# The last stage of a two-layer model: token order of the expert weights, and which engine normalises, takes the powers and splits the activations

## The reference, cut to what matters

```python
x = x + _L1_ffn_ref(_layernorm(x, axis=-1), ...)

shared = silu(x @ shared_w_gate.T) * (x @ shared_w_up.T) @ shared_w_down.T   # 352 wide
shared = shared * sigmoid(x @ shared_gate_w.T)
logits = x @ gate_w.T                          # 16 experts
rw, sel = top_k(softmax(logits), 2)
rw = rw / rw.sum(axis=-1, keepdims=True)
combine = zeros((N, 16)).at[arange(N)[:, None], sel].set(rw)
g, h = split(einsum('nd,edf->nef', x, w_gate_up), 2)      # 64 wide each
out = einsum('nef,efd,ne->nd', silu(g) * h, w_down, combine) + shared
```

## Time and profile before

| | us |
|---|---|
| median of 3 runs (2034.19 to 2035.87) | 2034.31 |
| the profiled execution, device time | 2034.19 |
| its span in the trace | 2032.0 |
| of that, the last stage from its first normalisation | 1781.3 to the end |
| ScalarE, busy in the whole span | 1498.5 |
| GpSimd, busy in the whole span | 899.9 |

### The profile page before, as it was taken

The page is one execution under the profiler, slowest core; times in us unless marked ns, Lnnn a source line. Parts: engine busy times, 40 slices in busy tenths (PEclk is TensorE's granted clock), DMA queues, the critical chain, the costliest instruction groups (busy, mean ns, idle before and its releaser), DMA issues. The chain is left out here.

```text
span 2032.0 us, 51069 instructions
## 1 busy us (share of the span) xinstructions
PE 1710.1 (84%) x13415; PEld 1396.7 (69%) x13415; DVE 1594.2 (78%) x5015; ACT 1498.5 (74%) x4147; POOL 899.9 (44%) x1335
## 2 busy tenths in 40 slices
PE   3599999999999999972530569999999889887997
PEld 3499999999999999951420246666666566575775
DVE  4798888888888888846688759999999778874664
ACT  3488888888888888846576369999999688763553
POOL 1554444444444444404155114444444277724554
PEclk8699999999999999985665779999999889978998
DMA  4366666666666666620000039999999710034654
GB/s 138 89 164 166 162 160 160 160 158 159 161 163 163 160 159 161 158 63 0 0 0 0 0 84 248 247 249 246 245 247 247 179 33 0 2 48 72 99 99 103
DMA packets 224923, 261.66 MB, mean 129 GB/s; under 512 B 25144, under 2 KB 178268, under 8 KB 224720
## 3 DMA queue, kind: packets, MB, share of 16 engines
q1 hardware_dynamic: 223366, 258.64, 51.7%
q10 hardware_dynamic: 1194, 1.58, 0.3%
q0 software_dynamic: 288, 0.56, 0.1%
HBM read 88.19 MB, written 4.74 MB: 46 GB/s over the span
## 5 line engine op out<-in xcount | busy, mean ns | idle before, releaser
L777 ACT ACTIVATE a_prob<-a_neg,a_nmax 128x289 f32<-128x289 f32 x512 | 268.0, 529 | 1.3 <-DVE a_nmax L704 1.0
L839 PE MATMUL a_out<-a_probT,a_xn 128*128 128x256 f32 x1024 | 265.4, 383 | 3.9 <-DMA a_probT<-a_blocks 2.3
L1709 ACT ACTIVATE b_prob<-b_neg,b_nmax 128x257 f32<-128x257 f32 x512 | 261.1, 516 | 4.9 <-DVE b_nmax L1660 4.5
L670 POOL TENSOR_TENSOR a_xn<-a_z,g 128x256 f32<-128x256 f32 x128 | 93.9, 734 | 383.5 <-DVE a_z L738 383.5
L829 PE MATMUL a_score<-a_xnT,a_qT 128*128 128x290 f32 x1536 | 252.6, 314 | 1.1 <-DVE a_qT L749 1.1
L704 DVE CUSTOM_DVE_ANT_0 a_neg<-a_score,a_bias 128x289 f32<-128x289 f32 x512 | 210.6, 458 | 40.5 <-PE a_score L829 36.0
L785 ACT ACTIVATE a_prob<-a_prob,a_rinv 128x289 f32<-128x289 f32 x512 | 232.1, 529 | 1.7 <-DVE a_rinv L754 1.7
L829 PEld LDWEIGHTS a_score<-a_xnT,a_qT 128*128 128x128 f32 x1536 | 221.9, 190 | 8.0 <-issue 1.6
L1660 DVE CUSTOM_DVE_ANT_0 b_neg<-b_score,b_bias 128x257 f32<-128x257 f32 x512 | 188.9, 422 | 32.7 <-PE b_score L1800 17.6
L839 PEld LDWEIGHTS a_out<-a_probT,a_xn 128*128 128x128 f32 x1024 | 176.8, 192 | 19.1 <-DMA a_probT<-a_blocks 2.9
L715 DVE STREAM_TRANSPOSE a_blocks<-a_prob 128x1024 f32<-128x1024 f32 x128 | 159.4, 1245 | 25.1 <-ACT a_prob L785 18.4
(11 more groups left out here) (480 smaller groups left out, 4551.7 us busy)
## 6 DMA issues: line engine op xcount, KB each, us to landing
a_probT<-a_blocks SPq DMA_DIRECT2D x512, 192.0 KB, 3.4
b_probT<-b_blocks SPq DMA_DIRECT2D x256, 256.0 KB, 4.7
a_raw<-in_ctx SPq DMA_DIRECT2D x128, 128.0 KB, 3.0
b_raw<-in_ctx SPq DMA_DIRECT2D x64, 256.0 KB, 4.2
m_wide<-expert_weights SPq DMA_DIRECT2D x128, 128.0 KB, 6.7
a_kept<-keep SPq DMA_DIRECT2D x32, 257.0 KB, 3.4
b_kept<-keep SPq DMA_DIRECT2D x32, 257.0 KB, 4.7
b_v_rows<-ctx_tail_values SPq DMA_DIRECT2D x32, 256.0 KB, 4.7
```

What stands on the lines that cost most here:

```text
L777: nc.scalar.activation(prob[:, par, grp, 0:KEYS0], neg[:, grp, :], ACT.Exp, bias=nmax[:, par, grp:grp + 1], scale=-1.0, accum_out=rsum[:, ...
L839: nc.tensor.matmul(out_ps[:, half, 0:2 * P], xn[:, j, kt, :], probT[:, u, 2 * half:2 * half + 2, kt, :], start=(kt == 0), stop=False)
L1709: nc.scalar.activation(prob[:, (j + 5) % 4, grp, :], neg[:, par, grp, :], ACT.Exp, bias=nmax[:, par, grp:grp + 1], scale=-1.0, accum_out=r ...
```

## The change

It does six things in `moe1`:

- Columns of `y` keep the tile order (no `by_batch` / `by_tile`), and so does `expert_weights`, now [17, 4096] in place of [4, 17, 1024]. A load of one expert's chunk reads one run of 512 floats in place of 4 runs of 128. A store writes, for each row and tile, a run of 32 floats, in place of one run for each row.
- DVE normalises all four tiles of each chunk; ACT normalises none, and `offset` goes.
- The low half of `y` is made by POOL, from `yT` and `y[:, HI]`, in place of DVE from PSUM. ACT's next copy into the same `yT` buffer waits for it; PE's next turn into the bank waits for ACT's copy alone.
- The exponentials become powers, e^gap and (1/e)^logit, on POOL (`gap_powers`, `gate_powers`), in place of ACT's `exps`.
- POOL takes the powers of part 0 after the low half of chunk 3, the gate powers of part 1 after its first `hidden[LO]`, and the gap powers of part 1 after its sixth.
- PE waits before the main loop until all `y[:, HI]` are written.

```diff
                 def store_weights(part):
                     tiles = tiles_of(part)
                     sp.wait_ge(comb_turned[part], 1)
-                    for i in range(BPT):
-                        sp.dma_start(k.comb_dram[i, :, tiles.start * L:tiles.stop * L],
-                                     combT[i * L:i * L + COLS, tiles, :].rearrange("e t l -> e (t l)")).then_inc(comb_stored, 16)
-                    sp.wait_ge(comb_stored, (part + 1) * BPT * 16)
+                    for i in range(P // L):
+                        sp.dma_start(k.comb_dram[:, tiles.start * P:tiles.stop * P].rearrange("e (t i l) -> e t i l", i=P // L, l=L)[:, :, i],
+                                     combT[i * L:i * L + COLS, tiles, :]).then_inc(comb_stored, 16)
+                    sp.wait_ge(comb_stored, (part + 1) * (P // L) * 16)
...
-                            sp.dma_start(wide[e * E_FF:(e + 1) * E_FF, p % 4, :].rearrange("p (i q) -> p i q", i=BPT),
-                                         weights_of(2 * p + e, c, E_FF)).then_inc(wide_loaded[p % 4], 16)
+                            sp.dma_start(wide[e * E_FF:(e + 1) * E_FF, p % 4, :],
+                                         k.comb_dram[2 * p + e:2 * p + e + 1, ds(c * CH, CH)].broadcast_to([E_FF, CH]))\
+                                .then_inc(wide_loaded[p % 4], 16)
...
-                    wait(pe, y_lo, c - 1)
+                    wait(pe, y_hi, c - 1)
...
-                def exps(part):
-                    tiles = tiles_of(part)
-                    act.wait_ge(chain[part], 12)
-                    nc.scalar.activation(powers[:, 0, tiles], gap[:, tiles], ACT.Exp)
-                    nc.scalar.activation(powers[:, 1, tiles], logits[:, tiles, E_N], ACT.Exp, scale=-1.0).then_inc(exped[part], 1)
...
+                    wait(act, y_lo, c - 1)
                     nc.scalar.activation(yT[:, c % 2, :], ln_ps[c % 2][:], ACT.Copy).then_inc(copied, 1)
-                    nc.scalar.activation(by_batch(y[:, HI, c * CH:(c + 1) * CH]), by_tile(ln_ps[c % 2][:]), ACT.Copy).then_inc(y_hi, 1)
+                    nc.scalar.activation(y[:, HI, c * CH:(c + 1) * CH], ln_ps[c % 2][:], ACT.Copy).then_inc(y_hi, 1)
...
+                def gap_powers(part):
+                    tiles = tiles_of(part)
+                    pool.wait_ge(chain[part], 12)
+                    nc.gpsimd.tensor_tensor(powers[:, 0, tiles], base[:, 0:1].broadcast_to([P, tiles.stop - tiles.start]), gap[:, tiles],
+                                            ALU.pow).then_inc(gap_power[part], 1)
...
+                for c in range(CHUNKS):
+                    pool.wait_ge(y_hi, c + 1)
+                    nc.gpsimd.tensor_tensor(y[:, LO, c * CH:(c + 1) * CH], yT[:, c % 2, :], y[:, HI, c * CH:(c + 1) * CH],
+                                            ALU.subtract).then_inc(y_lo, 1)
+                    if c == 3:
+                        gate_powers(0)
+                        gap_powers(0)
...
                     if op == 12:
-                        dve.wait_ge(exped[part], 1)
+                        dve.wait_ge(gap_power[part], 1)
+                        wait_apart(k, dve, gate_power[part], 1)
...
-                        nc.vector.tensor_tensor(by_tile(total[:]), by_batch(expert_ps[:]), by_batch(shared[:]), ALU.add).then_inc(total_ready, 1)
+                        nc.vector.tensor_tensor(total[:], expert_ps[:], shared[:], ALU.add).then_inc(total_ready, 1)
```

More of the change, by code:

```diff
@@ L10 @@
+import math
 from contextlib import ExitStack
@@ L2114, in moe1 @@
         powers = sb("m_powers", [P, 2, TILES])
-        offset = sb("m_offset", [P, TILES])
+        base = sb("m_base", [P, 2])
         comb, combT = sb("m_comb", [P, TILES, L]), sb("m_combT", [P, TILES, L])
@@ L2125, in moe1 @@
         shared, total = sb("m_shared_out", [P, CH]), sb("m_total", [P, CH])
-        z_act, z_dve, z_turned, copied, y_hi, y_lo, routed, gathered, offset_ready, comb_zeroed = (
-            sem(f"m_{n}") for n in ("z_act", "z_dve", "z_turned", "copied", "y_hi", "y_lo", "routed", "gathered", "offset_ready", "comb_zeroed"))
-        chain, exped, comb_turned = ([sem(f"m_{n}{part}") for part in range(2)] for n in ("chain", "exped", "comb_turned"))
+        z_ready, z_turned, copied, y_hi, y_lo, routed, gathered, base_ready, comb_zeroed = (
+            sem(f"m_{n}") for n in ("z_ready", "z_turned", "copied", "y_hi", "y_lo", "routed", "gathered", "base_ready", "comb_zeroed"))
+        chain, gap_power, gate_power, comb_turned = ([sem(f"m_{n}{part}") for part in range(2)] for n in (
+            "chain", "gap_power", "gate_power", "comb_turned"))
         comb_stored = sem("m_comb_stored")
@@ L2184, in store_weights @@
                     sp.wait_ge(comb_turned[part], 1)
-                    for i in range(BPT):
-                        sp.dma_start(k.comb_dram[i, :, tiles.start * L:tiles.stop * L],
-                                     combT[i * L:i * L + COLS, tiles, :].rearrange("e t l -> e (t l)")).then_inc(comb_stored, 16)
-                    sp.wait_ge(comb_stored, (part + 1) * BPT * 16)
-                def weights_of(e, c, rows):
-                    return k.comb_dram[:, e, ds(c * P, P)].unsqueeze(0).broadcast_to([rows, BPT, P])
+                    for i in range(P // L):
+                        sp.dma_start(k.comb_dram[:, tiles.start * P:tiles.stop * P].rearrange("e (t i l) -> e t i l", i=P // L, l=L)[:, :, i],
+                                     combT[i * L:i * L + COLS, tiles, :]).then_inc(comb_stored, 16)
+                    sp.wait_ge(comb_stored, (part + 1) * (P // L) * 16)
                 def chunk(c, u):
@@ L2196, in chunk @@
                         wait_apart(k, sp, shared_taken, c - 1)
-                    sp.dma_start(wide_share[:, u, :].rearrange("p (i q) -> p i q", i=BPT), weights_of(E_N, c, P)).then_inc(share_loaded[u], 16)
+                    sp.dma_start(wide_share[:, u, :], k.comb_dram[E_N:E_N + 1, ds(c * CH, CH)].broadcast_to([P, CH]))\
+                        .then_inc(share_loaded[u], 16)
                     for p in range(PAIRS):
@@ L2218, in turn_z @@
                 def turn_z(c):
-                    pe.wait_ge(z_act, c + 1)
-                    pe.wait_ge(z_dve, c + 1)
-                    wait(pe, y_lo, c - 1)
+                    pe.wait_ge(z_ready, c + 1)
+                    wait(pe, y_hi, c - 1)
                     for j in range(GRP):
@@ L2280, in _ @@
                         route(c - 1)
+                pe.wait_ge(y_hi, CHUNKS)
                 run(pe, step)
@@ L2297, in step @@
                         nc.scalar.activation(hidden[slot(i - 1)][0:r1, HI, :], full[0:r1, (i - 1) % 2, :], ACT.Copy).then_inc(hi_ready, 1)
-                    if isinstance(g, int) and n == 6:
-                        exps(1)
-                def exps(part):
-                    tiles = tiles_of(part)
-                    act.wait_ge(chain[part], 12)
-                    nc.scalar.activation(powers[:, 0, tiles], gap[:, tiles], ACT.Exp)
-                    nc.scalar.activation(powers[:, 1, tiles], logits[:, tiles, E_N], ACT.Exp, scale=-1.0).then_inc(exped[part], 1)
[L2307 to L2317, removed]
                 for c in range(CHUNKS):
@@ L2330, in _, with gate_powers @@
             def _(pool):
+                def gate_powers(part):
+                    tiles = tiles_of(part)
+                    pool.wait_ge(gathered, 1 if part == 0 else CHUNKS)
+                    nc.gpsimd.tensor_tensor(powers[:, 1, tiles], base[:, 1:2].broadcast_to([P, tiles.stop - tiles.start]), logits[:, tiles, E_N],
+                                            ALU.pow).then_inc(gate_power[part], 1)
+                def gap_powers(part):
+                    tiles = tiles_of(part)
+                    pool.wait_ge(chain[part], 12)
+                    nc.gpsimd.tensor_tensor(powers[:, 0, tiles], base[:, 0:1].broadcast_to([P, tiles.stop - tiles.start]), gap[:, tiles],
+                                            ALU.pow).then_inc(gap_power[part], 1)
                 def step(g, i):
@@ L2338, in step @@
                         nc.gpsimd.tensor_tensor(h[0:r1, LO, :], full[0:r1, 1 - u, :], h[0:r1, HI, :], ALU.subtract).then_inc(lo_ready, 1)
+                    if isinstance(g, int) and n == 1:
+                        gate_powers(1)
+                    if isinstance(g, int) and n == 6:
+                        gap_powers(1)
                 nc.gpsimd.memset(comb[:], 0.0).then_inc(comb_zeroed, 1)
+                nc.gpsimd.memset(base[:, 0:1], math.e)
+                nc.gpsimd.memset(base[:, 1:2], 1.0 / math.e).then_inc(base_ready, 1)
+                pool.wait_ge(base_ready, 1)
+                for c in range(CHUNKS):
[5 more added lines that the diff above has]
+                        gap_powers(0)
                 run(pool, step)
@@ L2346, in normalise @@
                     wait(dve, z_turned, c - 1)
-                    for j in range(2):
+                    for j in range(GRP):
                         t = c * GRP + j
```

(6 more changed lines are left out.)

6 lines of the change are left out of this document (removed).

## The result

The changed kernel takes 2052.88 us (median; 2049.58 to 2053.73, 4 runs) against 2035.09 (2034.19 to 2036.23, 4 runs): ratio 1.0086, 95% interval 1.0074 to 1.0097. It is slower, by some 17 us. The profiled execution has a span of 2049.1 us and a device time of 2050.88, against 2032.0 and 2034.19.

What follows compares the result with a forecast made beforehand. The store of part 1, on one DMA engine, was taken to lie openly on the path. Terms 28.1 - 3.9 - 2.0 + 0.5 + 3.0 = +25.7 on 2034.2 gave 2060 us, range 2030 to 2105.

Steps and rivals of the forecast that it cites:

- Where the kernel is bound: Last stage: DVE's 10.1 us wait for `m_wide` follows the store of part 1, each us longer costing one us.
- The store, +28.1: Store of part 1: 1904 packets at 20 ns on one DMA engine, 38.1 us against 10.0; ends 0 and +94.
- Short writes at double price: Rival: a 128-byte write makes the engine fetch and rewrite more, 55 ns a packet, kernel 2130 us; chance 0.13.
- Bytes only: Rival: one engine streams short packets as fast as long, store stays at 10.0 us, kernel 2032 us; chance 0.12.
- the spread store: Rival: all 16 engines share the store of part 1, 2.4 us, kernel 2024 us, faster; chance 0.07.
- First loads, -3.9: Chunk 1, store's landing to first pair: longer runs make it 5.5 us in place of 9.43; ends 0 and -5.
- Later loads, -2.0: DMA waits left beside the long one, 7.4 us, little of them on the path: -2.0 us, ends 0 and -7.4.
- Store of part 0, nothing: Store of part 0: 272 packets, 5.4 us in place of 1.9; costs nothing, with 5.9 us of cover.
- Prelude, +0.5: Prelude: DVE does four tiles in 1.45 us a chunk, PE stays the bound; +0.5 us, ends -0.5 and +1.5.
- Powers, +3.0, ends -1.5 and +8: Powers of part 1, ahead of its store: 3.5 us on POOL for 28 columns, about 2.0 us saved on ACT.

Runs made afterwards that it cites:

- E2: The changed kernel with each store of 17 rows cut in two DMAs, 16 rows and the 17th alone: ratio 0.9989 to the kernel before.
- E3: The changed kernel with each store cut in two DMAs of 16 floats of each run, 3808 packets of 64 bytes: 2074.96 us, 1.0188 to the kernel before.
- E4: The kernel before with only its stores cut in 16 rows and 1, runs of 3584 bytes kept: 2028.48 us, ratio 0.9963.
- E1: The kernel before with only the layout part of the change; engines, powers and queues as before: 2040.23 us, ratio 1.0016.
- E6: The changed kernel with the low half of `y` on DVE again, four tiles still on DVE, powers on POOL: ratio 1.0067 to the kernel before.
- E7: The changed kernel with two tiles of each chunk on ACT again, low half still on POOL: ratio 1.0054 to the kernel before.

## Why the prediction was right or wrong

The direction, the place and the range held; the size was 26 us forecast, 18 measured. That it came so near is partly luck: the store was off by 16 us one way, the prelude and the powers together by 9.6 the other.

- *Where the kernel is bound.* Right. The store of part 1 lies openly on the path: E2, E3 and E4 move it by -16.3, +22.4 and -7.6 us, and the stages follow with -20.7, +21.2 and -6.9 (the extra 4.4 of E2 goes with the clock, as said there).
- *The store, +28.1.* The term was mis-sized; it measured +12.1. The engine was right (one, E2), the count was right (1904), and so was "20 ns" as the engine time of a packet (18.3). The step that failed takes that as the time until the next one: "1904 x 20 = 38.1 us". The earlier trace rows had the warning in it: 84.4% of all engines' time for 3386 packets is engine time, and packets in flight together count twice in it (a little later in the same loads, 1632 to 1634 us, the share is 1.29 of what there is), while the earlier trace rows were of packets that follow each other. So the store landed 23.6 us after its issue and not 38, and the long wait was 17.8 us and not 35. What was needed is bytes over elapsed time; no row of before shows it for a short write.
- *Short writes at double price.* Wrong here: 128 bytes cost 9.4 to 11.7 ns by elapsed time, half or less of the 23 of 512 bytes (65 packets in 1.5 us, 1798.6 to 1800.1 before). The Trainium skill ("DMA: Bandwidth & Descriptors", section "Specifications") says read-modify-write under 512 bytes; if that happens, it doesn't double the price in these runs. What E3 shows is a lasting pace of about 11.8 ns for each packet.
- *Bytes only, and the spread store.* Both out: E3, and the steady 11 GB/s of the changed store. For the second the Trainium skill's rule (same page, section "Why a DMA increments its semaphore by 16 and not by 1", the largest divisor of the outermost size) is borne out by E2 and E4: 16 rows spread, 17 don't.
- *First loads, -3.9.* Measured -4.5. *Later loads, -2.0.* Measured -2.2, and -3.5 in E1. The closeness of the first is luck: the six kernels with this layout and an uncut store took from 165.8 to 167.4 us here, against 169.4, though nothing in this stretch differs between the six.
- *Store of part 0, nothing.* Right: it was issued at 1800.38, its loads began at 1804.71, and no wait for `m_wide` stands before chunk 1.
- *Prelude, +0.5.* Wrong: +4.0. The failed step is "PE stays the bound, and what others save is worth nothing": DVE's load was reckoned as four tiles in 1.45 us for a chunk, without the routing block, which stands in its queue ahead of the tiles that PE waits for (E6, +2.4), and POOL's subtraction was taken as work beside DVE's, while it stops DVE's operations (21.17 us busy where the operations alone are about 13.5; with half the tiles, E7, +1.0).
- *Powers, +3.0, ends -1.5 and +8.* Mis-sized, and past its own end: +9.1. A power of 28 columns took 4.79 to 5.18 us where 3.5 was taken, from ends of 0.7 and 7.1. The gate powers were priced at 0.5 "mostly under DVE's routing operations"; in fact PE waited 4.0 us behind them, since its next products stand behind the down product in its queue. The gain of 2.0 us on ACT that was set against this stands in no run by itself. And the term had no price for the clock, which fell from 0.93 to 0.75 over the stretch.
- The sum came nearer than its terms: 16.0 too much for the store, 9.6 too little for the prelude and the powers.

## What to carry to other kernels

Before a layout is changed, count what the transfer on the path becomes: its packets, and how many engines its outermost size lets it use. A store of 17 rows is worth cutting into 16 and 1 before anything else is tried, and only then does the better layout show. A share of DMA engines is not a pace: divide bytes by elapsed time for the same kind of transfer, and when an engine is priced as "beside the path", walk its queue for whatever stands ahead of the awaited instruction.

## What the runs showed of the hardware that was not expected

- Packets of 64 and of 128 bytes from SBUF to DRAM, on one DMA engine, by elapsed time: 7.0 and 9.4 ns each for the first 1 to 2 us (E3 and the changed kernel), then 11.8 and 11.7. Of 512 bytes 23 ns, of 3584 bytes 145 (72 packets in 10.45 us).
- A power on GpSimd takes 0.71 us for 2 columns, 1.03 to 1.12 for 4, 4.79 to 5.18 for 28: about 0.16 us for each column and 0.4 fixed.
- Beside a GpSimd subtraction on SBUF of 1.26 us, small VectorE operations on SBUF take 1.2 to 1.3 us in place of 0.2. Beside the powers they don't: between 1812.3 and 1817.4 us VectorE's operations take their usual 0.62 and 0.69 us, and the four tiles at 1792.74, beside a power of 1.05 us, their usual 1.11.
